# A two-layer decoder on one core: work moved at the last seams, and the second meeting of the engines between stages removed

## The reference, cut to what matters

```python
x = _layernorm(x + _L0_attn_ref(x, ...))        # windowed attention, 16 heads
x = _layernorm(x + _L0_xattn_ref(x, ctx_2048, mask))
x = _layernorm(x + _L0_ffn_ref(x, ...))         # 6 routed + 2 shared experts, two rounds of gates
x = _layernorm(x + _L1_attn_ref(x, ...))        # causal attention, 16 heads of 128
x = _layernorm(x + _L1_xattn_ref(x, ctx_2048, ctx_2048))   # 16 heads of 32, 1024 keys
x = _layernorm(x + _L1_ffn_ref(x, ...))

def _L1_ffn_ref(x, W1, Wg, W2, Ws1, Wsg, Ws2, gate_w, gate_b, biases):
    output = _expert_ffn(x, Ws1, Wsg, Ws2)                  # the shared expert, all tokens
    gate_probas = softmax(x @ gate_w + gate_b)
    topk_idxs = top_k(gate_probas + biases, 3)              # three of seven experts per token
    for e in range(7):
        output = output + _expert_ffn(x, W1[e], Wg[e], W2[e]) * w_e[..., None]
```

## Time and profile before

| | |
|---|---|
| median of three runs | 2057.42 us (2054.09 to 2058.44) |
| the profiled execution | 2055.97 us |
| its span, first to last instruction | 2054.2 us |
| PE busy | 1897.8 us (92%) |
| DVE busy | 1325.2 us (65%) |
| ACT busy | 1081.4 us (53%) |
| POOL busy | 641.8 us (31%) |
| mean granted TensorE clock | 0.956 |
| end of attn1, cross1, ffn1 (first meeting released) | 1400.3, 1682.1, 2053.3 us |

### The profile page before, as it was taken

How to read it: one execution, slowest core, us unless ns; L and a number is a source line. 1 busy time by engine, 2 the same in 40 slices (tenths; PEclk the granted TensorE clock), 3 DMA queues, 4 the chain that set the end, 5 groups by cost and what they waited for, 6 DMA issues and landing times. The chain is left out here.

```text
span 2054.2 us, 35547 instructions
## 1 busy us (share of the span) xinstructions
PE 1897.8 (92%) x12632; PEld 1167.8 (57%) x12632; DVE 1325.2 (65%) x2590; ACT 1081.4 (53%) x2139; POOL 641.8 (31%) x558
## 2 busy tenths in 40 slices
PE   7999889899999999989999999998888877999998
PEld 5666544578877888745455454553555543455553
DVE  6888765566566656768566585667899747454333
ACT  5887643443334333447355372663899872344333
POOL 5666311333333333121001010111676631222320
PEclk9999989999999999999999999996999768999999
DMA  6100035111110111142010100005400013666433
GB/s 218 48 27 2 1 114 201 43 49 39 51 51 26 52 41 56 49 122 65 21 42 21 41 21 0 1 1 124 92 2 3 2 45 136 210 183 166 123 69 97
DMA packets 107535, 136.31 MB, mean 66 GB/s; under 512 B 8408, under 2 KB 65880, under 8 KB 107376
## 3 DMA queue, kind: packets, MB, share of 16 engines
q1 hardware_dynamic: 100672, 118.66, 18.7%
q0 software_dynamic: 6720, 15.73, 3.9%
HBM read 108.28 MB, written 22.87 MB: 64 GB/s over the span
## 5 line engine op out<-in xcount | busy, mean ns | idle before, releaser
L1113 POOL TENSOR_TENSOR wl<-stage,wh 128x512 fp32r<-128x512 f32 x80 | 116.1, 1477 | 249.2 <-DVE wh L1108 249.2
L2967 POOL TENSOR_TENSOR PTl<-P,PTh 128x512 f16<-128x512 f32 (+2 forms) x160 | 148.8, 938 | 125.5 <-ACT PTh L3091 122.9
L1701 POOL TENSOR_TENSOR Zl<-z,Zh 128x512 f16<-128x512 f32 x32 | 51.2, 1601 | 416.0 <-ACT Zh L1861 416.0
L3090 ACT ACTIVATE P<-PS 128x512 f32<-128x512 f32 (+3 forms) x256 | 143.2, 559 | 46.9 <-PE PS L3035 43.1
L77 PE MATMUL PS<-XTh,wh 128*128 128x512 f16 x416 | 159.3, 383 | 2.8 <-PEq L130 2.8
L79 PE MATMUL PS<-XTh,wl 128*128 128x512 f16 x416 | 159.7, 384 | 0.0
L78 PE MATMUL PS<-XTl,wh 128*128 128x512 f16 x416 | 159.5, 383 | 0.0
L3091 ACT ACTIVATE PTh<-PS 128x512 f16<-128x512 f32 (+3 forms) x256 | 144.8, 566 | 0.0
L3107 DVE TENSOR_REDUCE M<-PS 128x1 f32<-128x640 f32 (+3 forms) x128 | 126.9, 1011 | 4.4 <-PE PS L3019 4.4
L1351 ACT ACTIVATE h<-PS,bup 128x512 f32<-128x512 f32 x64 | 44.1, 689 | 145.8 <-PE PS L79 145.2
L3035 PE MATMUL PS<-QS,KS 98*128 98x512 f16 (+3 forms) x256 | 101.3, 397 | 17.4 <-ACT PTh L3091 13.0
(11 more groups left out here) (377 smaller groups left out, 5819.1 us busy)
## 6 DMA issues: line engine op xcount, KB each, us to landing
stage<-in_ffn_W SPq DMA_DIRECT2D x18, 1024.0 KB, 5.3
stage<-in_ffn_Wg SPq DMA_DIRECT2D x9, 1024.0 KB, 5.5
stage<-in_ffn_Wup SPq DMA_DIRECT2D x16, 512.0 KB, 4.0
stage<-in_ffn_Wdn SPq DMA_DIRECT2D x16, 512.0 KB, 3.7
wq<-in_attn_wq SPq DMA_DIRECT2D x4, 1024.0 KB, 8.1
stage<-in_ctxT SPq DMA_DIRECT2D x8, 512.0 KB, 6.8
C<-in_ctx SPq DMA_DIRECT2D x8, 512.0 KB, 8.5
stage<-in_ffn_Wsw SPq DMA_DIRECT2D x16, 256.0 KB, 3.4
```

The costliest lines, as they stand in the source:

```text
L1113: self.c.nc.gpsimd.tensor_tensor(self.piece(self.low[q], ch), self.piece(self.stage, ch), plain(self.piece(self.high[q], ch)), ALU.subtrac ...
L1701: nc.gpsimd.tensor_tensor(Zl[:, hh, to], z32[:, uu % 2, :], Zh[:, hh, to], ALU.subtract).then_inc(z_lo, 1)
L2967: ops.tensor_tensor(PTl[:, (CT * n + kt) % RING, cols], P32[:, (CT * n + kt) % SLOTS, cols], PTh[:, (CT * n + kt) % RING, cols], ALU.subtr ...
L3090: nc.scalar.activation(P32[:, i % SLOTS, cols], c.PS[:, 4 + i % 2, cols], ACT.Exp, scale=SC)
```

## The change

Five edits.

**Meetings.** `free_sems` clears and frees the semaphores as before, but the second meeting is gone. The freed numbers are put at the end of the list of free ones.

**Output of attn1.** The first tile of a group waits for five low parts, and for the seventh only in front of its last head.

**Start of cross1.** 16 maxima are taken before the first exponential instead of 24. The first group's shift is made in two units of two heads (nine units instead of eight): the first is turned after three heads' maxima, the second in round 0. The missing eight maxima are taken in rounds 0 to 3, which then have 8, 6, 5 and 5 maxima instead of four each (`RAMP`). SP issues the loads of group 1, then the first shift rows, then the loads of groups 2 and 3, then two more shifts, and so on.

**End of cross1.** ACT does norm and `high` of the first four tiles, then of the last four; DVE does `low` of the first four before the moments of the last four. In rounds 22 to 31 the first two matrices of the next stage's shared expert are loaded into the key buffers of groups 1 and 2, when all exponentials of the first batch are made, and DVE splits them into the last slot of `WB`, which now has a fixed place at the end of SBUF (over buffers of the first batch): one DVE instruction at the head of each of rounds 27 to 30.

**Start of ffn1.** The shared expert is in slot 4, entry e in slot (e - 1) mod 5, the router's scratch in slot 3. SP starts with matrix 2; ACT does copy 0, copy 1, the exponential, then high part 2; DVE starts with `route.select`.

```diff
     def free_sems(self):
         self.nc.clear_and_free_semaphores(self.sems)
-        self.nc.all_engine_barrier()
+        freed = [s.num for s in self.sems]
+        free = [n for n in self.nc.free_semaphores if n not in freed]
+        self.nc.reset_free_semaphores(free + freed)
         self.sems = []
...
-        link(v.tensor_scalar(self.wrap[:], self.q[:], float(SLOTS), -float(SLOTS), ALU.is_ge, ALU.mult))
-        v.tensor_tensor(self.ring[:], self.q[:], self.wrap[:], ALU.add).then_inc(self.tabled, 1)
+        link(v.tensor_scalar(self.wrap[:], self.q[:], float(SLOTS + 1), -float(SLOTS), ALU.is_ge, ALU.mult))
+        v.scalar_tensor_tensor(out=self.ring[:], in0=self.q[:], scalar=-1.0, in1=self.wrap[:],
+                               op0=ALU.add, op1=ALU.add).then_inc(self.tabled, 1)
...
+class SharedFront:
...
+    def load(self, sp, i, stack):
+        sp.dma_start(self.staged(stack).rearrange("p (k n) -> p k n", k=KD),
+                     self.dram[i][NE - 1].rearrange("(k p) n -> p k n", p=P)).then_inc(self.arrived[i], 16)
...
+    def split_hi(self, dve, i, stack):
+        dve.wait_ge(self.arrived[i], 16)
+        self.c.nc.vector.tensor_scalar(self.part(2 * i), self.staged(stack), WS, None, ALU.mult).then_inc(self.hi, 1)
...
+    def split_lo(self, dve, i, stack):
+        dve.wait_ge(self.hi, i + 1)
+        self.c.nc.vector.scalar_tensor_tensor(out=self.part(2 * i + 1), in0=self.staged(stack), scalar=WS, in1=self.part(2 * i),
+                                              op0=ALU.mult, op1=ALU.subtract).then_inc(self.ready, 1)
...
         def _(sp):
-            for n in range(LOADS):
+            for w in w_in:
+                sp.sem_inc(w, 16)
+            for n in range(2, LOADS):
...
+            act.sem_inc(w_hi, 2)
             route.copy(act, 0)
-            split_hi(0)
             route.copy(act, 1)
-            split_hi(1)
+            route.exp(act)
             split_hi(2)
-            route.exp(act)
...
-            split_lo(0)
-            split_lo(1)
+            dve.wait_ge(shared.ready, 2)
+            dve.sem_inc(w_ready, 2)
             route.select(dve)
             split_lo(2)
...
                 if t == 0:
                     pe.wait_ge(w_lo, 4 * g + 4)
-                    pe.wait_ge(z_lo, U * g + U - 1)
+                    pe.wait_ge(z_lo, U * g + U - 3)
...
                 for hh in range(GH):
+                    if t == 0 and hh == GH - 1:
+                        pe.wait_ge(z_lo, U * g + U - 1)
...
+    FIRST = GS // 2
+    UNITS = [(0, 0, FIRST), (0, FIRST, GS)] + [(g, 0, GS) for g in range(1, N // GS)]
+    RAMP = ((0, 1, 2, 3, 4, 5, 6, 7), (0, 1, 3, 4, 5, 7), (0, 1, 3, 5, 7), (1, 3, 4, 5, 7))
...
+        def next_maximum(n, kt):
+
+            if n < len(RAMP):
+                if kt not in RAMP[n]:
+                    return None
+                m = QT * GS + sum(len(places) for places in RAMP[:n]) + RAMP[n].index(kt)
+                return divmod(m, QT)
+            return (n + LEAD, kt // 2) if kt % 2 == 1 and n + LEAD < N else None
...
+            load(range(1, 2))
             shift_rows(0)
...
+            load(range(2, half))
+            shift_rows(1)
+            shift_rows(2)
+            load(range(half, half + 2))
+            shift_rows(3)
+            load(range(half + 2, N // GS))
             cross.load_values(sp, 1)
...
+                if g >= N // GS - 2:
+                    sp.wait_ge(exp_done, CT * H)
+                    i = g - (N // GS - 2)
+                    shared.load(sp, i, KS[1 + i])
...
-            for n in range(LEAD):
+            for n in range(GS):
                 for qt in range(QT):
                     max_tile(n, qt)
-                if n == GS:
+                if n == FIRST:
                     turn_maxima(0, 0)
...
-            for t in range(NT + 1):
-                if t < NT:
-                    norm.root(act, t)
-                if t > 0:
-                    norm.normalize(act, t - 1)
-            for t in range(NT):
-                norm.high(act, t)
+            for first in (0, QT):
+                for t in range(first, first + QT + 1):
+                    if t < first + QT:
+                        norm.root(act, t)
+                    if t > first:
+                        norm.normalize(act, t - 1)
+                for t in range(first, first + QT):
+                    norm.high(act, t)
...
             for n in range(N + 2):
+                if N - 5 <= n < N - 1:
+                    i, lo = divmod(n - (N - 5), 2)
+                    if n == N - 5:
+                        dve.wait_ge(z_done, CT * H)
+                    (shared.split_lo if lo else shared.split_hi)(dve, i, KS[1 + i])
...
+            for t in range(QT):
+                norm.low(dve, t)
             for t in range(QT, NT):
                 norm.moments(dve, t)
```

More of the change, by code:

```diff
@@ L2885, in _, with phase_cross1 @@
                 norm.low(dve, t)
-def phase_cross1(c, cross, **end):
+def phase_cross1(c, cross, shared, **end):
     nc = c.nc
@@ L2957, in turned_bank, with turned_in, turned_through, maxima_through @@
             return c.PS[0:GS * QT, 6 + n % 2, QT * ZW:QT * ZW + P]
-        def turn_group(n):
+        def turned_in(n):
+            if n == 0:
+                return 1
             m = n + LEAD - 1
-            return m // GS if m % GS == GS - 1 and GS <= m < N else None
+            return m // GS + 1 if m % GS == GS - 1 and GS <= m < N else None
+        def turned_through(n):
+            return 1 + sum(turned_in(i) is not None for i in range(n + 1))
+        def maxima_through(u):
+            g, _, last = UNITS[u]
+            return QT * (GS * g + last)
+        def next_maximum(n, kt):
[5 more added lines that the diff above has]
+            return (n + LEAD, kt // 2) if kt % 2 == 1 and n + LEAD < N else None
         def low_part(engine, ops, n, kt, done):
@@ L2971, in _, with shift_rows, load @@
         def _(sp):
[L2972 to L2975, removed]
[L2977 to L2987 removed]
+            def shift_rows(u):
+                g, j, k = UNITS[u]
+                sp.wait_ge(m_lo, u + 1)
+                sp.dma_start(QS[g][R:R + 1, j:k], mh[0:(k - j) * QT]).then_inc(m_in, 16)
+                sp.dma_start(QS[g][R + 1:R + 2, j:k], ml[0:(k - j) * QT]).then_inc(m_in, 16)
+            half = N // GS // B
+            def load(groups):
+                for g in groups:
+                    cross.load_queries(sp, g)
+                    cross.load_keys(sp, g)
+            load(range(1, 2))
+            shift_rows(0)
+            load(range(2, half))
[4 more added lines that the diff above has]
+            load(range(half + 2, N // GS))
+            cross.load_values(sp, 1)
+            for u in range(4, len(UNITS)):
+                g = UNITS[u][0]
+                shift_rows(u)
+                if g >= N // GS - 2:
+                    sp.wait_ge(exp_done, CT * H)
+                    i = g - (N // GS - 2)
+                    shared.load(sp, i, KS[1 + i])
             norm.store(sp)
@@ L3029, in exp_tile @@
                 i = CT * n + kt
-                if kt == 0 and n % GS == 0:
-                    pe.wait_ge(m_in, 32 * (n // GS + 1))
+                if kt == 0 and (g, h) in [unit[0:2] for unit in UNITS]:
+                    pe.wait_ge(m_in, 32 * ([unit[0:2] for unit in UNITS].index((g, h)) + 1))
                 need(pe, exp_done, i - 1)
@@ L3048, in value_tile @@
                     need(pe, z_out, n - 1)
-                    pe.wait_ge(m_shift, 1 + sum(turn_group(i) is not None for i in range(n + 1)))
+                    pe.wait_ge(m_shift, turned_through(n))
                 hi, lo, slot = Vh[b][:, kt, h, :], Vl[b][:, kt, h * DV:(h + 1) * DV], (CT * n + kt) % RING
@@ L3154, in _ @@
             norm.factors(dve, NT - 1)
-            for t in range(NT):
+            for t in range(QT, NT):
                 norm.low(dve, t)
```

83 lines of the change are left out of this document (50 added, 33 removed).

## The result

The changed kernel has a median of 2027.85 us over four runs (2022.1 to 2029.04), the kernel before 2055.76 us beside it (2049.14 to 2058.44). The ratio is 0.9865, with a 95% interval from 0.9846 to 0.9883: 27.9 us less, where 20.5 were forecast and 2031 was the low end of the range. The profiled execution took 2027.0 us, of which 2025.2 are span: 29.0 less than the span before.

A forecast was written before the change was run, and what follows sets the result against it. PE, busy for 92% of the span, was taken as the bound, leaving only its idle time at stage seams to win. Terms 3.7 + 5.4 + 1.2 + 0 + 0 + 10.2 = 20.5 us gave 2036.9 us, range 2031 to 2044.

The forecast's parts named there:

- the failed step: Rounds 0 to 3 of cross1: eight added maxima and the ninth shift give DVE 36.7 us of work.
- Meetings: Five stage seams: 0.6 to 0.8 us each without the second meeting, 0.3 at the end; -3.7 us in sum.
- Output of attn1: attn1's output products: PE's wait for the seventh low part goes in four groups, no new wait at `turn(u, 1)`; -5.4 us.
- Start of cross1: Prelude and rounds 0 to 3: first exponential 8.9 us earlier, rounds longer; -1.2 us net, bounds -4.1 and +0.6.
- a value nearer the bad end: Start of cross1: -1.2 us chosen between 4.1 gain (DVE never waits) and 0.6 loss (DVE keeps 4.7 us waiting).
- pays in full: Rival, start of cross1: DVE waits for nothing in rounds 0 to 3, -4.1 instead of -1.2, 2034.0 us; chance 0.08.
- PE's 34.4 us at half clock: Rounds 0 to 3 of cross1: PE's work comes to 34.4 us with the added maxima at the prelude's clock of 0.50.
- Wrong if rounds 4 to 26 take other than 170 us: Sign in cross1: the forecast counts as wrong if rounds 4 to 26 take other than 170 us.
- Rounds 27 to 31: Late cross1: the shared expert's loads and DVE's 7.2 us of splits fit idle time; cost 0, or 7.2 without cover.
- Norm: End of cross1: second half starts 3.0 us later, last low ends about as before; 0, bounds -1.0 and +1.1.
- Start of ffn1: Front of ffn1: exponential moved ahead, line 565 10.3 us earlier; -10.2 us, bounds -10.3 and -5.
- half-gain rival: Rival, front of ffn1: lower PE clock or late matrix 2 leaves only -5 us, 2042.1 us; chance 0.12.

The follow-up runs named there:

- the whole: The changed kernel with all its parts, timed again in a later series against the kernel before: median 2027.73 us, ratio 0.9866.

## Why the prediction was right or wrong

The direction held, and so did most of the sums; 2027.85 us lies below the range because the terms for the start of cross1 and for the meetings were too small. The profile's 29.0 us exceed the 20.5 forecast by 8.5: 5.3 in cross1, 3.0 in attn1, 0.2 in the rest together. A part is the base: the median before was 2057.42 in the runs shown first and 2055.76 beside the result. No single term explains it: with the failed step put right the forecast would have been 2033 us, inside the range and still 5 us too long.

**Meetings (3.7 forecast, 5.1 measured alone, 6.6 in the whole).** The time between the releases is gained as put, 0.6 to 0.8 us at each seam. What the term left out is the clock: attn1 gains 2.6 to 2.9 us instead of 0.8, and ffn1 with the new front 1.9 instead of 0.6, as a 3.4 us stretch at the lower level disappears from each. That these stretches go with the meeting (or with the semaphore numbers changed beside it) is shown by the profiles; why they do isn't. The 0.3 us at the end were not there (0.7 us from the clear to the end of the span in both kernels).

**Output of attn1 (5.4; 6.4).** Right in kind; no wait opened at `turn(u, 1)`. The stage starts its later groups 1.34, 1.65, 1.68 and 1.50 us earlier, each some 0.1 to 0.2 more than the idle time put down. "5.6 less what four releases cost" should have been 5.6 and more: 6.2 to 6.5 by the stage's length.

**Start of cross1 (1.2; 5.9 in the whole).** This is the step that failed: "They add 8 x 1.0 us on DVE, and the ninth shift adds some 1.5 [...], so DVE has 36.7 us of work in these rounds". The first exponential comes 8.9 us earlier, as put, but rounds 0 to 3 are 3.9 us longer and not 7.7. DVE was busy for 32.65 us and not 36.7: its work grew by 5.4 us instead of 9.5 (32.6 to 33.0 us in all eleven profiles with four heads first). The 4.1 us between the two are made of four things: the durations that were added overlap, by 2.8 us after and 1.6 before (1.2); the twelve low parts take 8.0 us instead of 9.3 (1.3), which isn't explained; most of the last added maximum ends behind the first exponential of round 4 (0.9); and the shift adds 0.8 instead of 1.5 (0.7).

The choice that looked riskiest was right. "I take a value nearer the bad end" meant 39.6 - 36.7 = 2.9 us of waiting left out of 4.7, and 3.2 were left. The rival *pays in full*, given 0.08, said that DVE would wait for nothing; that didn't happen. The gain up to round 4, 8.9 - 3.9 = 5.0 us, is beyond the 4.1 that the forecast had as its best case, because both ends were worked out from the 36.7. PE's 34.4 us at half clock never came either: PE was busy for 27.8 to 30.4 us in rounds 0 to 3. In the eleven profiles with four heads first the clock rises 1.2 to 2.0 us after the first exponential, in the six with six heads 9.2 to 10.1 us after it, in the one with three 12.6. The forecast had no means to see that, but it mattered less than it seems, since 6.8 us more at the lower level went with 1.0 us. Rounds 4 to 26 add 1.3 us by the medians. "Wrong if rounds 4 to 26 take other than 170 us" named a number that isn't stable to begin with.

**Rounds 27 to 31 (0; a loss of 0.5 to 0.6).** The splits fit into DVE's idle time (busy for 26.98 of 35.54 us), though the four took 9.4 us instead of 7.2. What they slow is POOL, which the step didn't look at. POOL's rows in these rounds, in the changed kernel and in the one without the splits:

```profile
L3033 POOL TENSOR_TENSOR PTl<-P,PTh 128x512 f16<-128x512 f32 (+2 forms) x25 | 32.3, 1316 | 0.4 <-ACT PTh L3171 0.4
```

```profile
L2995 POOL TENSOR_TENSOR PTl<-P,PTh 128x512 f16<-128x512 f32 (+2 forms) x26 | 23.9, 926 | 10.1 <-ACT PTh L3128 10.1
```

Its 10.1 us of idle time covered nearly all of it; round 30 took 7.6 to 7.7 us instead of 7.0 in all eight profiles with the splits, and 7.0 in the ten without. There ACT's exponential at 1638.64 starts just behind the end of the POOL low part six tiles before it (1636.96 + 1.61), the one that has to free its slot. The Trainium skill (SBUF — State Buffer, section SBUF: two separate sides) says that a DVE operation with two inputs in SBUF and one of GpSimd exclude each other for a whole instruction. The trace agrees: beside the second split of a matrix, which has two such inputs, a POOL low part takes 2.47 and 2.72 us, where 1.16 is the longest without the splits. But low parts of 1.6 us stand behind the last split too, where they overlap DVE's own low parts.

**Norm (0; 0.6, not told from nothing).** The second half began 3.1 us later and the last low ended 17.0 us after the last exponential in both kernels, as worked out. With the splits in place the stage ends 0.4 us later behind the last exponential with the old order, in both profiles that have the two together.

**Start of ffn1 (10.2; 9.7 with the loss above taken off, 10.9 in the stage).** Right, step by step: exponential 1.3 us after its table load, `total` 10.9 us earlier, the first product of the 30 tiles at 58.5 us after the clear instead of 69.4, no wait for weights in the tiles. The half-gain rival didn't come.

**What stays open.** Alone, the early start gives 1.6 and 3.9 us over 24 timed executions; with the meetings gone it gives 6.0, in the whole 5.9. Its stage took 274.7 to 275.0 us in four of four profiles. Beside it stand 281.5 to 282.2 us in three profiles with the old start and the meetings, but 278.5 in the fourth, so the stage's own gain is between 3.5 and 7 us, and the kernel before may often be as quick as in its second profile. Or the stage is longer in some timed executions, which no profile met (the four profiled took 2047.1 to 2048.9 us, below the median of 2050.9 to 2051.2 of the timed ones), or the loss lies in another stage. The runs don't settle which. Nor is it settled what sets the moment at which the clock rises in cross1, why the second meeting brings one more half-clock stretch, or whether the order of the semaphore numbers has a part in that.

## What to carry to other kernels

The work of an engine in a stretch is its busy time, in which overlaps count once; instructions times their mean duration came out too high here, and what crosses the border of the stretch must be left out. A stretch that is re-ordered or shifted need not keep its clock: work the term out at both levels, and let neither stand for certain because the old order had it. When work is put into an engine's idle time, also check which other engine it can slow, and what cover that one has. Parts of a change at different seams should be measured undone from the whole as well as alone: here the four parts gave 20.9 us alone, with intervals of over 2 us each, undone from the whole 28.6, and the whole 27.5.

## What the runs showed of the hardware that was not expected

Taking out 0.6 to 0.8 us of standstill (and renumbering the semaphores) took a 3.4 us stretch of half clock away in attn1 (2.6 to 2.9 us in all). The same kernel's cross1 stage took 278.5 and 281.8 us in two executions with the same instructions, at a clock of 0.97 and 0.93 in rounds 4 to 26. The moment at which the clock rises in cross1 moved by 7 to 11 us with the number of maxima ahead of the first exponential, and not in one direction: 9.2 to 10.1 us after that exponential with 24, 1.2 to 2.0 with 16, 12.6 with 12.
